# Attention scores of eight heads by matmuls of 32 rows, four side by side, instead of matmuls of 128 rows over spread queries, with two accumulator banks fewer and a new order of all engines

## What is computed

```python
# block 1: windows of 8x8 tokens, 8 heads of 16 channels
normed = layernorm(win, ln1_g, ln1_b)                 # (windows, 64, 128)
q, k, v = heads(split(normed @ in_w.T + in_b, 3))
scores = einsum('bhsd,bhtd->bhst', q, k) / sqrt(16)
attn = softmax(scores, axis=-1)
o = einsum('bhst,bhtd->bhsd', attn, v)
win = win + o @ out_w.T + out_b
y = y + silu(layernorm(y, ln2_g, ln2_b) @ fc1_w.T + fc1_b) @ fc2_w.T + fc2_b
# block 2, xf = y as (batch, 128, 1024)
q, k, v = wq@xf + bq, wk@xf + bk, wv@xf + bv           # 64 channels
attn = einsum('bne,bem->bnm', q, k) / 1024
out = einsum('ce,bne->bcn', wo, einsum('bnm,bme->bne', attn, v)) + bo + xf
```

## Time and profile before

| | before |
|---|---|
| median of 3 runs | 365.99 us (365.3 to 366.18) |
| the profiled execution | 366.59 us, its span 364.8 us |
| PE busy | 348.3 us, 95% of the span |
| weight loads (PEld) | 299.3 us, 82% |
| DVE busy | 285.1 us, 78% |
| ACT busy | 245.6 us, 67% |
| POOL busy | 166.9 us, 46% |

### The profile page before, as it was taken

How to read it: one execution, slowest core, us unless ns; L and a number is a source line. 1 busy time by engine, 2 the same in 40 slices (tenths; PEclk the granted TensorE clock), 3 DMA queues, 4 the chain that set the end, 5 groups by cost and what they waited for, 6 DMA issues and landing times. The chain is left out here.

```text
span 364.8 us, 9920 instructions
## 1 busy us (share of the span) xinstructions
PE 348.3 (95%) x3424; PEld 299.3 (82%) x3424; DVE 285.1 (78%) x850; ACT 245.6 (67%) x449; POOL 166.9 (46%) x177
## 2 busy tenths in 40 slices
PE   7899899999999999999999999999999999999875
PEld 6788788888888888888888888878888888878563
DVE  5676888888788878798788888888788878867652
ACT  5557776775959477674968658684877659684360
POOL 6513575444455434635445433646444443622430
PEclk9999999999999999999999999999999999999995
DMA  4242130303222131302123031212123031210011
GB/s 133 67 100 63 33 97 4 91 29 82 76 60 72 29 86 58 86 29 72 63 67 86 14 101 58 70 45 58 58 72 101 0 86 58 60 31 2 0 60 58
DMA packets 31859, 21.99 MB, mean 60 GB/s; under 512 B 22432, under 2 KB 23776, under 8 KB 31840
## 3 DMA queue, kind: packets, MB, share of 16 engines
q1 hardware_dynamic: 31744, 21.62, 21.7%
q10 hardware_dynamic: 96, 0.13, 0.1%
HBM read 4.95 MB, written 4.19 MB: 25 GB/s over the span
## 5 line engine op out<-in xcount | busy, mean ns | idle before, releaser
L526 POOL TENSOR_TENSOR hid_l<-hid,hid_h 128x512 fp32r<-128x512 f32 x30 | 40.4, 1369 | 37.1 <-ACT hid_h L1136 35.3
L706 PE MATMUL p_score<-kd_h,qd_h 128*128 128x128 f32 (+1 forms) x512 | 55.8, 252 | 1.6 <-DMA qd_h<-q_h 1.5
L706 PEld LDWEIGHTS p_score<-kd_h,qd_h 128*128 128x128 f32 (+1 forms) x512 | 49.9, 163 | 6.9 <-DVE row_max L1344 1.7
L1102 ACT ACTIVATE probs<-p_scoreT 128x512 f32<-128x512 f32 x64 | 38.6, 603 | 24.5 <-PE p_scoreT L729 24.4
L1344 DVE TENSOR_REDUCE row_max<-p_score 128x8 f32<-128x512 f32 x64 | 44.0, 687 | 14.1 <-PE p_score L706 14.0
L744 PEld LDWEIGHTS p_attn<-vd,probs 128*64 128x64 f32 x1024 | 36.2, 139 | 16.2 <-issue 9.0
L744 PE MATMUL p_attn<-vd,probs 128*64 128x34 f32 x1024 | 45.4, 244 | 1.7 <-ACT probs L1102 1.7
L531 POOL TENSOR_TENSOR y_l<-y,y_h 128x512 fp32r<-128x512 f32 x15 | 19.3, 1285 | 60.2 <-ACT y_h L1116 60.2
L518 POOL TENSOR_SCALAR kd_l<-k_l,head_a 128x512 fp32r<-128x512 f32 x15 | 23.6, 1572 | 35.7 <-DVE k_l L1326 21.3
L725 PE MATMUL p_scoreT<-qd_h,kd_h 128*128 128x256 f32 x128 | 39.5, 309 | 0.0
L510 POOL TENSOR_TENSOR rstd<-rstd,minus_half 128x4 f32<-128x4 f32 (+1 forms) x33 | 35.5, 1075 | 2.7
(11 more groups left out here) (262 smaller groups left out, 915.5 us busy)
## 6 DMA issues: line engine op xcount, KB each, us to landing
qd_l<-q_l SPq DMA_DIRECT2D x64, 64.0 KB, 2.0
vd<-v_tok SPq DMA_DIRECT2D x64, 64.0 KB, 2.2
qd_h<-q_h SPq DMA_DIRECT2D x62, 64.0 KB, 2.0
out<-out_sb SPq DMA_DIRECT2D x15, 256.0 KB, 2.0
x_in<-in_x SPq DMA_DIRECT2D x14, 256.0 KB, 2.7
x_first<-in_x SPq DMA_DIRECT2D x2, 256.0 KB, 2.8
fc_rows<-in_L_conv_fc_w SPq DMA_DIRECT2D x2, 128.0 KB, 2.6
out<-out_sb SPq DMA_DIRECT2D x2, 128.0 KB, 2.1
```

Source lines behind the costliest of these rows:

```text
L526: pool.tensor_tensor(hid_l[:, t], hid[:, t], hid_h[:, t].bitcast(F32), ALU.subtract).then_inc(hid_low[t], 1)
L706: last = pe.matmul(p_score[0:rows, 2 * KEYS * j:2 * KEYS * (j + 1)], qd_h[:, h.par, j, 2 * KEYS * p:2 * KEYS * p + rows], kd_h[:, h.par, 2 ...
L1102: act.activation(probs[:, p % 2], p_scoreT[:].rearrange("row (win j q) -> row win j q", win=2, j=QUADS), ACT.Exp, scale=SCORE_SCALE).then_ ...
```

## The change

**Scores over 32 rows.** Each matmul of `b_score` and `b_scoreT` now takes only the 32 rows of head pair j from `q_h`, `q_l`, `kd_h` and `kd_l`, and writes to a bank of its own, bank j of `p_s`. Four of them, j = 0 to 3, use disjoint rows of the array. `p_s` is four banks; the rough scores are columns 0 to 127 of each, the transposed ones columns 128 to 255. `b_score` stays at eight matmuls a pair (128 weight columns, 128 moving), `b_scoreT` goes from six matmuls of 256 moving columns to 24 of 64. To keep the two windows of a pair apart, `q_h` gets a block of zeros behind each window's queries, and the two windows accumulate. The four bf16 matmuls of the maximum stay as they are, over 128 rows.

**No spread queries.** `qd_h`, `qd_l`, their DMAs, their waits and their zero fills go; `q_h` and `q_l` are double buffered instead.

**Banks.** `p_s` takes four banks, so `p_a` is one bank and `p_d` is gone. In the loop `p_a` holds in turn the input transposes, the normalised transposes, queries, keys and values of a half, and each waits until the one before is read: `a_k` for `q_high` and `q_low`, `a_v` for `k_high` and `k_low`. The d functions use `p_c[1]` and, for the second half of an image, `p_attn`. As the two kinds of scores share banks, `b_max` of pair p now waits for the exponential of pair p-1, and `b_score` of pair p for that of pair p-2.

**New order.** The calls of all engines' `step` and `epilogue` are rearranged. Core of the diff:

```diff
             def b_score(h, p):
                 if p == 0:
-                    pe.wait_ge(q_high_dma, h.n(times=16 * QUADS))
+                    pe.wait_ge(q_high, h.n())
 ...
                 else:
                     pe.wait_ge(max_ready[p - 1], h.n())
-                for j in range(QUADS):
-                    for win, rows in ((1, 2 * KEYS), (0, KEYS)):
-                        last = pe.matmul(p_score[0:rows, 2 * KEYS * j:2 * KEYS * (j + 1)],
-                                         qd_h[:, h.par, j, 2 * KEYS * p:2 * KEYS * p + rows],
-                                         kd_h[:, h.par, 2 * p + win], start=True, stop=True)
+                    if p > 1:
+                        pe.wait_ge(probs_ready[p - 2], h.n())
+                flat = q_h[:, h.par].rearrange("p win two k -> p (win two k)")
+                for win in range(2):
+                    start = 2 * KEYS * (2 * p + win) - KEYS * win
+                    for j in range(QUADS):
+                        rows = slice(32 * j, 32 * j + 32)
+                        last = pe.matmul(p_score[:, j], flat[rows, start:start + 2 * KEYS],
+                                         kd_h[rows, h.par, 2 * p + win], start=win == 0, stop=win == 1)
...
             def b_scoreT(h, p):
...
-                    for k, (kd, qd) in enumerate(((kd_h, qd_h), (kd_h, qd_l), (kd_l, qd_h))):
-                        pe.matmul(dst[:, win], kd[:, h.par, window], qd[:, h.par, :, KEYS * window:KEYS * (window + 1)],
-                                  start=win == 0 and k == 0, stop=False, skip_group_check=True)
+                    for k, (kd, q) in enumerate(((kd_h, q_high_part), (kd_h, q_low_part), (kd_l, q_high_part))):
+                        for j in range(QUADS):
+                            rows = slice(32 * j, 32 * j + 32)
+                            pe.matmul(p_scoreT[:, j, KEYS * win:KEYS * (win + 1)], kd[rows, h.par, window], q[rows],
+                                      start=win == 0 and k == 0, stop=False, skip_group_check=True)
...
             def c_fc1(h, t, final=None):
...
+                    if final:
+                        pe.wait_ge(fin_kept[0], final.image(-1))
...
-            def b_attn(h, p):
+            def b_attn(h, p, final=None):
                 pe.wait_ge(probs_ready[p], h.n())
+                if final:
+                    pe.wait_ge(fin_kept[1], final.image(-1))
...
             def b_max(h, p):
                 dve.wait_ge(score_ready[p], h.n())
+                if p:
+                    dve.wait_ge(probs_ready[p - 1], h.n())
```

More of the change, by code:

```diff
@@ L438, in step_even @@
                     load_x(loop.half(2))
-                spread_q(loop.half(1))
                 spread_v(loop.half(1))
-                if not c:
-                    load_late()
             def step_odd(loop, more, d):
@@ L446, in step_odd @@
                     load_x(loop.half(3))
-                    spread_q(loop.half(2))
                     spread_v(loop.half(2))
@@ L810, in d_kvT @@
                 dst = d_bank(loop, c)
-                if loop.follows(c - 1) and dst is p_d:
-                    pe.wait_ge(fin_kept[1], loop.image(c - 1))
+                if dst is p_a:
+                    pe.wait_ge(v_kept, 2 * IMAGES)
                 for n in tiles:
@@ L890, in step @@
                     c_project(c)
-                b_score(b, 2)
-                if not with_c:
-                    b_scoreT(b, 1)
                 if with_tail:
@@ L896, in step @@
                 b_attn(b, 0)
+                if with_a and with_c:
+                    a_q(a)
                 if with_c:
                     c_yT(c)
+                b_score(b, 2)
+                b_scoreT(b, 1)
                 if with_tail:
@@ L901, in step @@
                 if with_a and with_c:
-                    a_q(a)
                     a_k(a)
-                if with_c:
-                    b_scoreT(b, 1)
-                b_score(b, 3)
+                if not with_c:
+                    a_v(a)
+                b_attn(b, 1)
                 if with_d:
                     d_kvT(loop, -1)
-                b_attn(b, 1)
-                if with_a:
-                    a_v(a)
+                b_score(b, 3)
+                b_scoreT(b, 2)
+                if with_c:
+                    c_back(c)
                 if with_d:
                     d_bT(loop, -1)
-                b_scoreT(b, 2)
+                if with_a and with_c:
+                    a_v(a)
+                b_attn(b, 2)
                 if with_d:
@@ L1146, in d_out @@
                 for v in range(2):
-                    last = act.activation(in_rows(out_sb[:, half, :], v), in_windows(p_d[:], v), ACT.Identity,
+                    last = act.activation(in_rows(out_sb[:, half, :], v), in_windows(final_bank(loop, c, half)[:], v), ACT.Identity,
                                           bias=d_col[:, 0:1])
@@ L1195, in step @@
                     c_yn(c)
+                if with_a and with_c:
+                    a_v(a)
                 if with_a:
                     a_k_block(a, 1)
-                if with_d:
-                    d_out(loop, -1, 0)
                 b_exp(b, 3)
```

279 lines of the change are left out of this document (129 added, 150 removed).

## The result

The kernel after takes 446.8 us (median of four runs, 440.5 to 461.7), the kernel before 366.0 us in the same session (365.3 to 366.2): 1.21 times as long, 95% interval 1.198 to 1.226. This ratio leaves out the two slower runs of the kernel after, 447.1 and 461.7 us; by the medians it is 1.22. The profiled execution took 446.4 us with a span of 444.6 us.

The account below looks back on a forecast made before the run. PE's instruction stream was taken as the bound; new waits add 51.3 us over six rounds: 364.8 + 51.3 + 2.7 + 0.6 + 2.85 + 1.0 - 1.6 = 421.7, with 1.2 to the median 423 us. Walk's bounds 395 and 450; range 372 to 465.

Parts of the forecast that it names:

- PE as the bound of before, slack of DVE and ACT as the measure: Loop: PE, 95% busy, sets the time; DVE and ACT have some 3.5 and 5 to 7 us slack a half.
- Rival 1: Loop: queues hide the new order, no wait reaches PE, which stays the bound; faster, 353 us; chance 0.12.
- Rival 2: Loop: only the waits at the image's end or those at the halves' start bite; 380 to 396 us; chance 0.15.
- Side by side: `b_score`, `b_scoreT`: four row groups load together, 0.11 us a round; gain 2.0 us a half.
- Layout changes: PE between 32-row and full-size matmuls: 8 new changes at 0.33 us each cost 1.3 us a half.
- The walk through an even half: Even half through four queues: late `xn` and a 2.1 us wait for `c_norm`; 22.0 instead of 19.15 us, +2.85.
- The odd half: Same walk, odd half: waits at `d_kvT`, `m_l` and output passes; 28.2 instead of 22.53 us, +5.7.
- theory 2: Supposition from the experiments, not the prediction: PE's clock falls where little of its time passes columns, whether waiting or loading weights.
- The shapes: PE's stream in the loop: gain of 2.0 less 1.3 us for layout changes, 0.7 us shorter a half.

Follow-up runs that it names:

- e8: The kernel after with 24 filler matmuls ahead of `c_back` in each half and 16 ahead of `d_final` 0 in each odd half: 423.3 us.
- e3: The kernel after in order and banks, with score matmuls of the kernel before in number and size: 418.9 us.
- e4: The kernel after with every matmul of `b_score` and of `b_scoreT`'s three passes over 128 rows instead of 32, same number and columns: 582.2 us.
- e9: The kernel before with each of `b_scoreT`'s six matmuls of 256 moving columns taken as four of 64: 536.6 us.
- e1: The kernel after with 24 filler matmuls of 128x128 ahead of `c_back` in each half: 426.9 us.
- e11: The kernel after with `c_back` behind `d_bT` and `a_v`, the d order of before, DVE's `d_bT` ahead of `c_yn`, 12 filler matmuls ahead of `a_v`: 407.7 us.
- e7: The kernel after with later `c_back`, the d order of before, `d_kvT` behind `b_scoreT` 2, and the score matmuls of e3: 412.0 us.
- e12: e11 with the score matmuls of the kernel before in number and size: 407.0 us.
- e6: The kernel after with later `c_back`, the d order of before and `d_kvT` behind `b_scoreT` 2, new shapes kept: 429.1 us.

## Why the prediction came out as it did

The forecast was 423 us, slower, by waits; measured were 446.8. The direction and the mechanism of the waits were right, and the sizes of the largest of them. The missing 24 us are a term that the sum doesn't have, made smaller by waits that came out less than forecast.

By stretches, after less before, with the forecast in brackets: preparation -2.1 (-1.6), first half -0.3 (+0.6), second half +5.5 (+2.7), loop +73.3 (+51.3), even half behind it +1.3 (+2.85), epilogue +2.1 (+1.0). Of the 22.9 us missing in the span, 22.0 are in the loop and 2.8 in the second half, the two stretches where the clock was lowest.

- **PE as the bound of before, slack of DVE and ACT as the measure:** right. Rival 1 (queues hide the order) fell: ACT's `xn` is there for DVE only 4.7 us into the half (below), far behind the 2.9 that this rival needs. Rival 2 (only one of the two sets of waits bites, 380 to 396) fell too: `yn_tok` stands beside `kv_tok` and `m_l` in the waits above.
- **Side by side:** right, `b_score` 0.27 (forecast 0.23), `b_scoreT` 0.75 (0.68). The prediction's estimate from a figure of the Trainium skill (TensorE: Matmul & The Clock Gate, Measured speedup vs the span model) was 0.29 and 0.86; both measured values lie between that estimate and the one from `b_attn`'s rows.
- **Layout changes:** forecast 0.33 for in and out. At the full clock the step from the last round of `b_scoreT` to the first full-size matmul is 0.22 us (381.32 to 381.54) where a round takes 0.11, so 0.11 for the way out; the way in can't be read apart from it, so the 0.33 is neither confirmed nor refuted. The gap agrees with the drain at a change of tiling mode that the Trainium skill states (TensorEngine Tiling, Key Properties).
- **The walk through an even half:** forecast `xn` at 4.65, DVE idle until 4.75, `c_back` waiting 2.1 us. Timeline of DVE in the even half that starts at 379.12:

```profile
383.86 0.76 DVE L1297 TENSOR_TENSOR xn_l<-p_a,xn_h 128x256 fp32r<-128x256 f32 x2 [1.92 <-ACT xn L1050]
384.53 0.68 DVE L1336 TENSOR_REDUCE row_max<-p_s 128x8 f32<-128x512 f32 x1
...
390.20 0.66 DVE L1336 TENSOR_REDUCE row_max<-p_s 128x8 f32<-128x512 f32 x1
...
392.79 1.36 DVE L1279 TENSOR_SCALAR yn_tok<-p_c,mv,rstd 128x128 f32<-128x128 f32 x4
```

  DVE starts `xn_l` at 4.74 (forecast 4.75) after 1.92 us idle (1.9), `b_max` 1 ends at 6.09 (6.1), `b_max` 2 at 11.74 (12.05), `c_norm` at 15.0 (15.5), `c_back` starts at 15.09 (15.6) after a wait of 1.89 us (2.1). The rest of the half takes 5.3 us where the walk had 6.4. In the loop, where the inputs of the next half are transposed too, even halves at the full clock took 21.35 and 21.57 us (22.0).
- **The odd half:** at their longest `kv_tok` 0.8 (forecast 1.0), `m_l` 1.2 (1.15), ahead of `b_attn` 3 1.0 (1.1). These are not met in full each time: `m_l` has 3.8 us in six waits. The wait ahead of `c_fc1` 1 for the first output pass, forecast at 0.6, shows only once in the kernel after, 0.4 us. The full-clock round of e8 is 49.4 us, forecast 50.2; six rounds give 6 x (49.4 - 41.6) = 47 against 51.3. So the waits were forecast 4.5 us too large in the loop, and the clock's share of it is some 26 us (73.3 less 47), as an estimate from these two runs. That the time still fell inside the range is luck: its upper bound, 450, was set for 0.1 us more at each link of a half, and that is not what happened.
- **What failed** is the unspoken step that PE's instructions keep the durations that they have in the earlier trace rows, all at clock 1.00. The prediction moved PE from 95% to far less and put 24 small matmuls in place of six long ones, and either was a reason to ask for the granted clock; neither the sum nor a rival did. 28% of the loop ran at 1.2 GHz. e8 wins back 23.5 us by filler alone and ends at 423.3.
- **My first account of it failed too.** I took the waits for the cause. e3 stands still for 38 of 300 us at a clock of 1.00, e4 for 13 of 350 us at 0.87, e9 not at all at 0.89. In the order of before, many loads with few columns each were enough to bring the clock down (e9); in the changed order waits alone were not (e3), and the new shapes with the waits were. That matmuls of no use raise it (e1, e8, e11) also speaks against a limit that answers to too much work. All this is in line with theory 2. It is not shown that nothing else plays a part: e7's clock of 0.97 with the old shapes has no test of its own, and the new shapes were never run without the waits. The Trainium skill (TensorE: Matmul & The Clock Gate, What's actually happening) says that activity releases the throttle. The traces agree in that the fillers raised the clock, but PE's busy share in the profile doesn't tell it: 389.99 of 390 us in e9, at 0.89.
- **The shapes** were forecast to be worth 0.7 us a half. In a fixed order they are worth nothing (e11 407.7, e12 407.0 us) or cost 17 to 28 us (e6 against e7, after against e3), with the lower clock on the side of the new ones.

What is left open: e11's 41 us above the kernel before. PE's waits of e11 are many and in the loop none over 1.0 us, and moves of one of them made others; no run took all away.

## What to carry to other kernels

When an edit makes TensorE's matmuls shorter or leaves it waiting, ask what the granted clock will be and read it first in the profile after; a sum over durations taken at the full clock leaves out what a fall of the clock costs. Here the other engines had some 3.5 us of slack a half, and the order of the queues was worth far more (53 us, with the banks) than the engine time saved: walk one half through all queues before believing a saving. And a wait that is moved is seldom gone: see which other waits grow in its place before counting the gain.

## What the runs showed of the hardware that I had not expected

- TensorE's clock fell in a loop in which it was busy 389.99 of 390 us (e9: 0.89), and stayed at 1.00 in one in which it stood still for 38 of 300 us (e3). e9 differs from the kernel before, which stayed at 1.00, only in 64 moving columns behind each weight load of `b_scoreT` instead of 256.
- Matmuls of no use, 24 of 128 columns in a wait of each half, raised the clock from 0.87 to 0.94 and made the kernel 20 us faster; 16 more in each odd half gave 0.96 and 23.5 us.
- At the lower clock weight-bound groups slow down as well: `b_attn` 1.07 against 0.71 us, four transposes 1.06 against 0.66.
- Runs of a kernel whose clock falls scatter by 1 to 5% (after: 440.5 us at a clock of 0.88, 461.7 at 0.83), those of one that keeps it by 0.1 to 0.3% (e3, e12), the kernel before by 0.2 to 0.9% over its sessions; e7 and e11, at 0.96 to 0.98, by 0.6 to 0.7%.
